# Part of batch 0's preparation moved to VectorE, half of its transfers issued from ScalarE's queue, and due times of its own for that stage

## The reference

```
mod = silu(c) @ wmod                 # six vectors per batch: sa, ca, ga, sb, cb, gb
h = layernorm(x) * (1 + ca) + sa
x_dbl = h @ W_x.T                    # 64 for the step size, 16 for B, 16 for C
dt = softplus(dt_raw @ W_dt.T + b_dt)
state = exp(dt * A) * state + (dt * h) * B     # for 16 states per feature, along the tokens
y = sum over states of state * C;  x = x + ga * (y + h * D)
h = layernorm(x) * (1 + cb) + sb
gates = the two largest of softmax(h @ Wg) of 8 experts, made to sum to 1
x = x + gb * sum over the two experts of gate * (h @ We + be)
```

## Time and profile before

| | |
|---|---|
| median of 3 runs | 1220.47 us |
| lowest, highest | 1218.09, 1220.68 us |
| the profiled execution's own time | 1216.74 us |
| its span, first to last instruction | 1214.9 us |
| busy VectorE, GpSimd, TensorE, ScalarE | 1023.8, 1001.4, 932.1, 715.2 us |
| granted TensorE clock, mean over the span | 0.881 |
| first scan starts | 50.63 us |

### The profile page before, as it was taken

One profiled execution on the slowest core, in us unless ns is written; L12 is line 12 of the kernel. 1 busy time (PEld: TensorE's weight loads), 2 busy tenths in 40 slices (PEclk: granted clock), 3 DMA queues, 4 the chain that ended last, 5 costly groups with the idle time before them and its releaser, 6 DMA issues. The chain is left out here.

```text
span 1214.9 us, 13519 instructions
## 1 busy us (share of the span) xinstructions
PE 932.1 (77%) x4235; PEld 590.9 (49%) x4235; DVE 1023.8 (84%) x826; ACT 715.2 (59%) x1412; POOL 1001.4 (82%) x357
## 2 busy tenths in 40 slices
PE   5335444578878888698877898788968897789998
PEld 4101111245644556455554565355644565456786
DVE  2399999999899989998999989998999989995110
ACT  4864569556874669557865588466955367331200
POOL 1376676689997999799997999799979999797453
PEclk9656766599998998999998999898998999889899
DMA  5607160364427171555346261727144443611132
GB/s 164 155 19 168 40 138 1 89 173 101 125 70 208 46 190 36 135 145 134 92 104 175 65 169 46 171 91 182 52 114 132 113 115 84 166 45 47 57 100 61
DMA packets 90552, 131.21 MB, mean 108 GB/s; under 512 B 13536, under 2 KB 73512, under 8 KB 90480
## 3 DMA queue, kind: packets, MB, share of 16 engines
q1 hardware_dynamic: 90480, 130.34, 41.2%
HBM read 54.50 MB, written 8.65 MB: 52 GB/s over the span
## 5 line engine op out<-in xcount | busy, mean ns | idle before, releaser
L965 POOL TENSOR_TENSOR h<-h,Cr 128x2048 f32<-128x2048 f32 x129 | 582.4, 4517 | 97.0 <-DVE h L835 53.5
L835 DVE TENSOR_TENSOR_SCAN h<-av,ps 128x1024 f32<-128x1024 f32 x256 | 584.7, 2284 | 16.6 <-DVE ps L828 0.9
L588 PE MATMUL ps<-xg,we 128*128 128x256 f32 x2048 | 501.1, 401 | 21.3 <-POOL xg L1002 18.9
L588 PEld LDWEIGHTS ps<-xg,we 128*128 128x128 f32 x2048 | 402.0, 201 | 119.1 <-POOL xg L1002 33.8
L1002 POOL TENSOR_TENSOR xg<-h2T,gbc 128x1024 f32<-128x1024 f32 x128 | 304.3, 2383 | 64.8 <-DMA gbc<-gates 30.7
L828 DVE TENSOR_TENSOR ps<-ps,dd 128x1024 f32<-128x1024 f32 x256 | 315.4, 1232 | 46.7 <-PE ps L473 26.1
L631 ACT ACTIVATE av<-dd,An 128x1024 f32<-128x1024 f32 x256 | 289.5, 1141 | 69.7 <-DVE h L835 50.9
L492 PE MATMUL ps<-h,gam 128*32 128x512 f32 x1024 | 141.2, 674 | 44.1 <-POOL h L965 33.4
L685 ACT ACTIVATE Cr<-ps 128x512 f32<-128x512 f32 x64 | 38.0, 596 | 99.8 <-PE ps L533 79.9
L473 PE MATMUL ps<-S,sel 64*128 64x512 f32 x128 | 51.7, 487 | 48.3 <-DVE ps L828 48.3
L492 PEld LDWEIGHTS ps<-h,gam 128*32 128x32 f32 x1024 | 29.2, 117 | 119.8 <-issue 77.4
(11 more groups left out here) (100 smaller groups left out, 855.9 us busy)
## 6 DMA issues: line engine op xcount, KB each, us to landing
dd<-src SPq DMA_DIRECT2D x512, 128.0 KB, 2.4
gbc<-gates SPq DMA_DIRECT2D x128, 256.0 KB, 3.7
X<-in_x SPq DMA_DIRECT2D x8, 1024.0 KB, 8.2
out<-X SPq DMA_DIRECT2D x32, 256.0 KB, 3.3
XN<-in_x SPq DMA_DIRECT2D x7, 1024.0 KB, 7.9
we<-in_We SPq DMA_DIRECT2D x2, 1024.0 KB, 8.7
XN<-in_x SPq DMA_DIRECT2D x2, 512.0 KB, 5.2
Cr<-in_wmod SPq DMA_DIRECT2D x1, 1024.0 KB, 5.3
```

Of the source, the lines that this page charges most:

```text
L588: e = pe.matmul(bk[:, m * 256:(m + 1) * 256], we[:, hf, 2 * ep + e2, m * P:(m + 1) * P], xg[:, i % XG, e2, hf], start=(ep == e2 == m == hf ...
L835: dve.tensor_tensor_scan(h[:, u % HS], av[:, u % AS], wide(BP), 0.0, ALU.mult, ALU.add).then_inc(s_scan, 1)
L965: pool.tensor_tensor(hu, hu, Cr[:, q:q + 1].to_broadcast([P, n, L]), ALU.mult).then_inc(s_ch, n)
```

## The change

For batch 0 alone: VectorE norms blocks 4 to 7 (`xh`), reads out the transposes of the second half of the tokens, and does the three operations of `dt` for the first half of the features (hf = 0). ScalarE's queue issues the 16 transfers `ddu` of hf = 0. The stage of batch 0 has due times of its own: the names in `AT` that end in H, and `dtE`, `dduE`, `ddusE`. `late` moves `stat`, `xh`, `rstd` and `rsb` of batch 1 by 8.8 units. The other numbers of the table are set anew too, most by less than 1 unit in the stages of batches 0 to 5, by more for the last batches.

```diff
-AT = dict(exp=0.41, mul=-0.14, scan=0.75, ch=8.26, Bs=0.81, y=7.93, stat0=-4.62, stat0s=0.74, rstd0=1.29,
...
+AT = dict(late=8.8, dduE=32.18, ddusE=0.16, dtE=2.1, exp=0.41, mul=-0.14, scan=0.83, ch=8.27, Bs=0.63, y=7.87,
+          stat0=-4.61, stat0s=0.74, rstd0=0.72, rsb0=1.59, xh0=4.14, xh0s=0.03, xT0=15.42, xT0h=1.27,
...
+          xh0H=-1.95, xh0sH=1.64, rstd0H=-4.79, rsb0H=0.93, xT0H=6.43, xT0hH=1.59, xTsH=2.75, rxT0H=2.02,
+          wxH=6.2, rwxH=0.7, SH=4.33, gamH=27.64, dl0H=19.63, dl1H=38.05, dlsH=3.16, rdlH=0.53, corrH=1.35,
+          dtH=7.73, CH=28.81, CSH=2.12, CcH=1.8, rCH=0.94, ddtH=31.05, ddtsH=2.44, dduH=35.5, ddusH=0.0,
+          stat0H=-14.35, stat0sH=3.45, ldxH=27.43)
 def before(b, t, put):
+    times = AT if b else {n[:-1]: t for n, t in AT.items() if n[-1] == "H"}
+    late = AT["late"] if b == 1 else 0.0
...
-            put(t + AT["stat0"] + k * AT["stat0s"], "stat", 0, b, k)
-        put(t + AT["xh0"] + k * AT["xh0s"], "xh", 0, b, k)
+            put(t + late + times["stat0"] + k * times["stat0s"], "stat", 0, b, k)
+        put(t + late + times["xh0"] + k * times["xh0s"], "xh", 0, b, k)
...
+            put(s + (AT["dtE"] if b == hf == 0 else times["dt"]), "dt", b, hf, c)
...
+            if b == hf == 0:
+                put(s + AT["dduE"] + AT["ddusE"] * j, "ddu", 0, j)
...
+        def early(s):
+            return s[:3] == ("xh", 0, 0) and s[3] >= 4 or s[:5] == ("read", "xT", 0, 0, 1) or s[:3] == ("dt", 0, 0)
...
-                elif s[0] == "ddu":
+                elif s[0] == "ddu" and s[1]:
...
-                    pe.wait_ge(s_xh[w], 8 * b + 4 * c + 4)
+                    if w == b == 0 and c:
+                        pe.wait_ge(s_xd, 4)
+                    else:
+                        pe.wait_ge(s_xh[w], 8 * b + 4 * c + (0 if b and not w else 4))
...
+                elif s[:2] == ("ddu", 0):
+                    j = s[2]
+                    act.wait_ge(s_dtu, 2)
+                    for nl in range(4):
+                        act.dma_start(dd[32 * nl:32 * nl + 32, j, 1], src[32 * j:32 * j + 32, 1]).then_inc(s_ddu[j], 16)
...
+                elif s[0] == "xh" and early(s):
+                    k = s[3]
+                    if k == 4:
+                        dve.wait_ge(s_rs[0], 1)
+                    dve.tensor_scalar(XN[:, k], XN[:, k], rs[:, 0, 4, k:k + 1], rs[:, 0, 5, k:k + 1], ALU.mult, ALU.add).then_inc(s_xd, 1)
+                elif s[0] == "read" and early(s):
+                    hf, use = s[5], s[1:]
+                    done(dve, use)
+                    release(dve.tensor_scalar(hT[:, 0, hf, CH:], mb(use), md[:, 2 + hf, 0:1], md[:, hf, 0:1], ALU.mult, ALU.add), use)
+                elif s[0] == "dt" and early(s):
+                    c = s[3]
+                    cs = slice(c * CH, (c + 1) * CH)
+                    emptied(dve, ("dl", 0, 0, c))
+                    dve.tensor_tensor(src[:, 1, cs], src[:, 1, cs], sp_t[:, 1], ALU.subtract).then_inc(s_lp, 1)
+                    dve.wait_ge(s_lp, c + 1)
+                    dve.tensor_tensor(src[:, 0, cs], src[:, 1, cs], src[:, 0, cs], ALU.add).then_inc(s_dt, 1)
+                    dve.wait_ge(s_dt, c + 1)
+                    emptied(dve, ("xT", 0, 0, c, 0))
+                    dve.tensor_tensor(src[:, 1, cs], src[:, 0, cs], hT[:, 0, 0, cs], ALU.mult).then_inc(s_dtu, 1)
...
-                elif s[0] == "dt":
+                elif s[0] == "dt" and not early(s):
```

More of the change, by code:

```diff
@@ new lines @@
+AT = dict(late=8.8, dduE=32.18, ddusE=0.16, dtE=2.1, exp=0.41, mul=-0.14, scan=0.83, ch=8.27, Bs=0.63, y=7.87,
+          stat0=-4.61, stat0s=0.74, rstd0=0.72, rsb0=1.59, xh0=4.14, xh0s=0.03, xT0=15.42, xT0h=1.27,
+          xTs=2.34, rxT0=0.3, wx=4.17, rwx=1.64, S=0.01, ldx=29.35, gam=20.53, dl0=20.66, dl1=36.03, dls=3.22,
+          rdl=0.66, corr=0.19, dt=7.52, C=25.68, CS=2.8, Cc=0.79, rC=0.39, ddt=37.71, ddts=1.56, ddu=37.99,
+          ddus=2.02, zs=2.87, ldx2=31.87, z=4.99, zX=-0.89, zd=2.25, stat1=6.82, stat1s=0.34, rstd1=9.53,
+          rsb1=0.98, xh1=11.01, xh1s=0.0, xh1g=1.46, xT1=11.82, xT1h=0.17, xT1s=1.36, rxT1=0.57, lg=13.68,
+          rlg=0.71, lT=0.95, soft=0.48, softe=0.3, top=1.09, gT=2.52, rgT=0.59, gw=11.5, gr=35.22, xg=23.28,
+          xgs=1.78, gl=-2.87, f=-3.14, fE=0.75, o=2.42, oX=1.89, out=13.69, md1=-55.56, gates=-53.1,
+          ga=-19.87, bn0=-110.74, bn0s=1.79, stat1A=5.82, stat1B=11.38, stat1sA=1.5, stat1sB=7.75,
+          rstd1A=3.59, rstd1B=9.2, rsb1A=2.78, rsb1B=2.24, xh1A=8.35, xh1B=43.37, xh1sA=0.0, xh1sB=2.42,
+          xh1gA=34.12, xh1gB=7.57, xT1A=9.31, xT1B=30.95, xT1hA=0.0, xT1hB=12.76, xT1sA=1.43, xT1sB=4.9,
+          rxT1A=-0.69, rxT1B=27.91, lgA=10.45, lgB=78.97, rlgA=-1.55, rlgB=-3.18, lTA=0.92, lTB=9.51,
+          softA=2.14, softB=-5.6, softeA=-1.4, softeB=10.02, topA=3.55, topB=5.15, gTA=1.79, gTB=18.98,
+          rgTA=-0.6, rgTB=2.95, gwA=14.18, gwB=34.72, grA=49.74, grB=115.72, xgA=36.06, xgB=160.95, xgsA=8.75,
+          xgsB=16.41, glA=7.55, glB=29.63, fA=32.58, fB=-11.74, fEA=63.67, fEB=33.05, oA=22.32, oB=61.86,
+          oXA=-3.35, oXB=64.36, outA=46.39, outB=74.14, stat1P=6.9, stat1sP=0.31, rstd1P=9.96, rsb1P=0.0,
+          xh1P=11.6, xh1sP=0.02, xh1gP=1.64, xT1P=11.64, xT1hP=0.58, xT1sP=1.58, rxT1P=0.28, lgP=14.46,
+          rlgP=0.11, lTP=0.12, softP=-0.56, softeP=1.41, topP=-0.43, gTP=0.59, rgTP=1.31, gwP=10.42,
+          grP=32.32, xgP=21.51, xgsP=1.82, glP=-3.74, fP=-3.42, fEP=-0.48, oP=4.87, oXP=10.3, outP=68.01,
+          xh0H=-1.95, xh0sH=1.64, rstd0H=-4.79, rsb0H=0.93, xT0H=6.43, xT0hH=1.59, xTsH=2.75, rxT0H=2.02,
+          wxH=6.2, rwxH=0.7, SH=4.33, gamH=27.64, dl0H=19.63, dl1H=38.05, dlsH=3.16, rdlH=0.53, corrH=1.35,
+          dtH=7.73, CH=28.81, CSH=2.12, CcH=1.8, rCH=0.94, ddtH=31.05, ddtsH=2.44, dduH=35.5, ddusH=0.0,
+          stat0H=-14.35, stat0sH=3.45, ldxH=27.43)
@@ L56, in before @@
         if b:
-            put(t + AT["stat0"] + k * AT["stat0s"], "stat", 0, b, k)
-        put(t + AT["xh0"] + k * AT["xh0s"], "xh", 0, b, k)
-    put(t + AT["rstd0"], "rstd", 0, b)
-    put(t + AT["rstd0"] + AT["rsb0"], "rsb", 0, b)
+            put(t + late + times["stat0"] + k * times["stat0s"], "stat", 0, b, k)
+        put(t + late + times["xh0"] + k * times["xh0s"], "xh", 0, b, k)
+    put(t + late + times["rstd0"], "rstd", 0, b)
+    put(t + late + times["rstd0"] + times["rsb0"], "rsb", 0, b)
@@ L61, in before @@
     for c in range(2):
-        s = t + AT["xT0"] + AT["xTs"] * c
+        s = t + times["xT0"] + times["xTs"] * c
         for hf in range(2):
[L64 to L70, removed]
+            put(s + times["xT0h"] * hf, "xT", 0, b, c, hf)
+            put(s + times["xT0h"] * hf + times["rxT0"], "read", "xT", 0, b, c, hf)
@@ L71, in before @@
+        put(s + times["wx"], "wx", b, c)
+        put(s + times["wx"] + times["rwx"], "read", "wx", b, c)
+        put(s + times["wx"] + times["S"], "S", b, c)
+    put(t + times["ldx"], "ldx", b + 1)
+    put(t + times["gam"], "gam", b)
     for hf in range(2):
         for c in range(2):
-            s = t + AT["dl1" if hf else "dl0"] + AT["dls"] * c
+            s = t + times["dl1" if hf else "dl0"] + times["dls"] * c
             put(s, "dl", b, hf, c)
-            put(s + AT["rdl"], "read", "dl", b, hf, c)
@@ L76, in before @@
-            put(s + AT["corr"], "corr", b, hf, c)
-            put(s + AT["dt"], "dt", b, hf, c)
+            put(s + times["rdl"], "read", "dl", b, hf, c)
+            put(s + times["corr"], "corr", b, hf, c)
+            put(s + (AT["dtE"] if b == hf == 0 else times["dt"]), "dt", b, hf, c)
         s = t + 16 * hf
         for j in range(NJ):
-            put(s + AT["ddt"] + AT["ddts"] * j, "ddt", 2 * b + hf, j)
-            put(s + AT["ddu"] + AT["ddus"] * j, "ddu", 2 * b + hf, j)
+            put(s + times["ddt"] + times["ddts"] * j, "ddt", 2 * b + hf, j)
@@ L82, in before @@
+            if b == hf == 0:
+                put(s + AT["dduE"] + AT["ddusE"] * j, "ddu", 0, j)
+            else:
+                put(s + times["ddu"] + times["ddus"] * j, "ddu", 2 * b + hf, j)
     for q in range(NQ):
         for c in range(2):
-            s = t + AT["C"] + AT["CS"] * q + AT["Cc"] * c
+            s = t + times["C"] + times["CS"] * q + times["Cc"] * c
             put(s, "C", b, q, c)
-            put(s + AT["rC"], "read", "C", b, q, c)
+            put(s + times["rC"], "read", "C", b, q, c)
@@ L295, in adaln_block @@
                                                 for n in ("s_mean", "s_sq", "s_ln", "s_rd", "s_rs", "s_xh"))
+        s_xd = sem("s_xd")
         s_ga, s_gam = sem("s_ga"), sem("s_gam")
@@ L407, in _ @@
                         sp.dma_start(dd[32 * nl:32 * nl + 32, j, 0], src[32 * j:32 * j + 32, 0]).then_inc(s_ddt[j], 16)
-                elif s[0] == "ddu":
+                elif s[0] == "ddu" and s[1]:
                     _, H, j = s
                     sp.wait_ge(s_dtu, 2 * H + 2)
-                    if H:
```

(4 more changed lines are left out.)

## The result

| | before | changed |
|---|---|---|
| median of 12 runs each (lowest to highest) | 1218.29 us (1215.52 to 1221.18) | 1222.78 us (1219.29 to 1225.78) |
| profiled execution, its span | 1216.74, 1214.9 us | 1222.52, 1220.7 us |

The ratio of the times is 1.0041, 95% interval 1.0027 to 1.0055: the change costs 5.0 us (3.3 to 6.7; the medians are 4.5 apart). Forecast was a gain of 3.3.

A forecast was written before the change was run, and what follows sets the result against it. It took the kernel as bound by a fed VectorE line from scan 3 to 1085 us. The start's terms summed to scan 3 ending at 64.3 instead of 67.65 us, so 1220.47 - 3.3 = 1217.2 us, range 1213.0 to 1221.0.

The forecast's parts named there:

- part 5: Batch 0's 32 transfers: product ones issued from ScalarE at 0.63 us each; second queue gives 1.8 us, not 10.
- rival B: ScalarE held by its issues: change stops paying at 0.91 us each; at 1.2, 4.6 us slower, 1225.1; chance 0.10.
- Part 1: Batch 0's norm and read-out partly on VectorE: costs 0.3 us rather than wins, written as 0.
- Part 2: Both projections ahead of the step sizes on TensorE: ScalarE's step sizes end at 38.2, gain 0.3 us.
- Part 3: Step sizes' tail on VectorE, 0.7 us per operation: step sizes ready 1.6 us earlier, product 2.2 us earlier.
- Part 4: Eight statistics of batch 1 moved by 8.8 units: first spread of B ready before the data; cost 0.
- Scan 3's end: End of the fourth recurrence step: 64.3 us against 67.65 before, 3.35 us earlier.
- Passing through one to one: After scan 3, a microsecond won at the start moves everything behind it by one.
- The time forecast: Whole kernel: 1220.47 - 3.3 = 1217.2 us, chance 0.40.
- The other due times: Rest of the retuned table, few steps moved: taken as 0, with one wait of about 2.7 us to each side.

The follow-up runs named there:

- the second profile: One more profiled execution each of the unaltered kernel before and changed kernel; scan 20 started 1.2 us earlier and 0.7 us later than in their first profiles.
- the first experiment: Changed kernel with batch 0's 16 product transfers issued from SyncE again, each four behind the step-size four of the same part; median 1216.76 us.
- the new due times alone: Kernel before with the new values of the old names of the table and nothing else; ratio 1.0034 to the kernel before.
- the run with parts 0 and 3: Changed kernel, but ScalarE issues product transfers j = 0 and 3 only, SyncE the other 24, old due times outside batch 0's stage; median 1217.58 us.

## Why the prediction was wrong

It was wrong in sign. The failed step is in part 5: "the nearest is SyncE's 0.63, I take it". An issue on ScalarE takes 1.11 us there. Through the prediction's own chain that is 16 x 0.48 = 7.7 us more ahead of exp 1. Exp 1 started 5.4 us later than forecast (58.47 against 53.1), because three other terms were together some 2.4 us too long: the product was ready at 40.47 and not 41.1, exp 0 had no 0.7 us left to wait for its data behind the long issues, and its 1.15 us did not hold the issues behind it (the ninth starts at 49.51, exp 0 at 49.49).

The mechanism was rival B's, which was given 0.10, and its bound of 0.91 us per issue was passed. That B's 4.6 us slower is near the 4.5 between the medians is partly luck. With 1.11 us in B's own formula scan 3 ends at 70.8, 3.2 us later than before. Measured were 1.7 us (69.33 against 67.65) in the first pair of profiles and 4.6 (71.07 against 66.52) in the second.

What makes this instructive is that the same part had the right number and used it for one thing only. It worked out that the engines were nearly full and that 32 transfers would take 18.4 us; they took 18.7. It let the landing times obey that and the issues not. But two queues that issue at 0.63 us offer a transfer every 0.32 us, and the engines take one every 0.58 (18.4 / 32), and the excess has to stand somewhere. The runs show where: on the issuing engines. SyncE has nothing else to do there; ScalarE had exp 0 and exp 1 to do. The argument against B, that 2 KB and 128 KB transfers have one issue price, came from a stretch with one queue, in which the engines never fell behind, and could not tell.

Point by point:

- Part 1 (norm and read-out, 0): VectorE's four norms took 1.38 us and ended at 23.89, and the projection started at 25.77 against 25.73, as if nothing was lost. Against the profile of before that starts as early, it costs 1.1 us. The term was mis-sized: it compared VectorE's norms with ScalarE's in an execution in which ScalarE's came 1.1 us late.
- Part 2 (0.3 us gained, 38.2): better. ScalarE's step sizes ended at 36.88 + 0.59 = 37.47. The two projections took 4.46 us together, the level of the clock rising within them. In the second profile the level rose later, they took 5.43, and the first transfer went out at 40.81.
- Part 3: an operation of VectorE took 0.69 us as taken; first transfer at 39.74 against 40.4 forecast (40.81 in the second profile). The forecast compared with the kernel before, where c1's projection came late enough to hide GpSimd's queue; with the projections first, GpSimd would have been late by 1.2 us more, which was missed.
- Part 4 (0): no wait of VectorE on batch 1's statistics is in the changed kernel's profile; the first spread of B was ready long before its data.
- Scan 3's end: 64.3 forecast, 69.33 measured; with the issues on SyncE 65.90.
- Passing through one to one: fits the loss, not shown for a gain. Changed against before it is 2.7 us at scan 20 in the first pair of profiles, 4.5 in the second, and 5.0 by the ratio; the first experiment against the changed kernel is 4.5 at scan 20 and 5.6 by the ratios. The kernels with an early scan 20 are no faster that can be told. What follows scan 20 goes with TensorE's granted clock: over the 13 profiles the rest of the span runs from 1084.0 us (clock 0.880, the kernel before) to 1090.1 (0.868, the first experiment), correlation -0.79, and -0.90 without the new due times alone (1092.3 at 0.871). A difference of 1 or 2 us in the start drowns in that.
- The time forecast, 1217.2: it rested on a median of three runs, 1220.47; the median of 12 is 1218.29.
- The other due times (0, a wait to each side): neutral in the changed kernel, 4.1 us in the kernel before. Not settled.

## What to carry to other kernels

Before half of a row of transfers goes to a second queue, divide the bytes by what the DMA engines move when full. Here one queue already kept them 0.88 busy; the second gave 1.5 us of 20.2, and the excess came back as longer issues on both queues. So a compute engine should issue only what it can pay for before its next due work, and transfers wanted late should not be sent beside those wanted now: in the run with parts 0 and 3 that put off mul 2 by 2.4 us. Where a bound on throughput is found, it has to be applied to every step that feeds it. And before two profiles are compared step by step, look whether they start alike: here one load that landed 1.1 us later made a loss of 1.1 us look like none.

## What was not expected of the hardware

- An issue's price is not fixed: 0.63 us with room in the engines, for 2 KB and 128 KB transfers alike, and 1.11 us (ScalarE) and 1.09 (SyncE) in the mean when both queues together keep them 0.98 busy. It is not held at once: SyncE's first four took 2.42 us in the changed kernel too.
- Two executions of one program differ by 1 us by the time the first transfers go out, here once by a load that landed later and once by a clock level that rose later. So a start must not be judged to less than that from single profiles.
- From run to run the time follows the mean granted clock of TensorE. Over 178 runs of ten programs, each against its own mean, a run with 0.01 less clock is 3.5 us longer (correlation -0.72; in the new due times alone there is none). VectorE's line is fed by TensorE at the batch boundaries, which would explain it but was not tested.
